# A recommendation model on one core: copied rows in a buffer per step, gathers that read the row numbers in place, and two more slots copied row by row

## What is computed

```python
x = jax.nn.relu(dense @ Wb0 + bb0)
x = jax.nn.relu(x @ Wb1 + bb1)
d = jax.nn.relu(x @ Wb2 + bb2)
sp = emb[jnp.arange(NUM_TABLES)[None, :], sparse_idx]
T = jnp.concatenate([sp, d[:, None, :]], axis=1)
Z = jnp.einsum('bnd,bmd->bnm', T, T)
li, lj = np.tril_indices(NUM_TABLES + 1, -1)
h = jnp.concatenate([d, Z[:, li, lj]], axis=1)
h = jax.nn.relu(h @ Wt0 + bt0)
h = jax.nn.relu(h @ Wt1 + bt1)
p = jax.nn.sigmoid(h @ Wt2 + bt2)
```

## Time and profile before

| quantity | value |
|---|---|
| median of three runs | 532.41 us |
| the profiled execution | 532.94 us |
| its span, first to last instruction | 530.9 us |
| outside the span | 2.0 us |
| POOL busy | 379.9 us (72%) |
| PE busy | 307.7 us (58%) |
| DVE busy | 245.5 us (46%) |
| ACT busy | 13.8 us (3%) |
| mean granted clock of TensorE | 0.72 |

### The profile page before, as it was taken

The page is one execution under the profiler, slowest core; times in us unless marked ns, Lnnn a source line. Parts: engine busy times, 40 slices in busy tenths (PEclk is TensorE's granted clock), DMA queues, the critical chain, the costliest instruction groups (busy, mean ns, idle before and its releaser), DMA issues.

```text
span 530.9 us, 12271 instructions
## 1 busy us (share of the span) xinstructions
PE 307.7 (58%) x3370; PEld 228.0 (43%) x3370; DVE 245.5 (46%) x375; ACT 13.8 (3%) x23; POOL 379.9 (72%) x406
## 2 busy tenths in 40 slices
PE   3799983774372732637436274366245744489776
PEld 1233432762262621626225252365124632377665
DVE  5435766644463344545246352376254732532220
ACT  1000000000000000000000000000000000021201
POOL 5777777777777777777777777777777777777710
PEclk9998895776667655777557775669567776579587
DMA  6445424444344433443344442444334443333310
GB/s 200 39 28 30 28 30 27 30 30 29 29 30 29 28 28 28 30 29 27 29 28 28 28 30 27 29 28 28 28 28 29 28 28 27 27 28 26 29 11 1
DMA packets 19968, 16.88 MB, mean 32 GB/s; under 512 B 11683, under 2 KB 12972, under 8 KB 19897
## 3 DMA queue, kind: packets, MB, share of 16 engines
q0 software_dynamic: 12800, 13.13, 31.8%
q1 hardware_dynamic: 4378, 2.68, 4.6%
q10 hardware_dynamic: 2732, 0.51, 3.4%
HBM read 16.28 MB, written 0.01 MB: 31 GB/s over the span
## 4 chain that ended last, share of the span: by engine, by line
POOL 50%; issue 20%; DMA 15%; PE 9%; DVE 6%; POOLq 0%; ACT 0%; DVEq 0%; ACTq 0%
POOL rows L307 50%; DMA rows<-in_emb,idx_step 14%; PE ps_t L343 3%; DVE vecs_mv L702 3%; PE ps_turn L351 1%; PE ps_turn L365 1%; PE ps_gram L334 1%; PE ps_feat L334 1%; PE ps_t L477 1%; DMA idx_raw<-in_idx 1%; PE ps_t L446 1%; PE ps_gram L419 1%; DVE hb L659 1%; DVE vecs_st L702 0%; PE ps_feat L446 0%
## 5 line engine op out<-in xcount | busy, mean ns | idle before, releaser
L307 POOL DMA_INDIRECT rows<-in_emb,idx_step x400 | 378.3, 946 | 126.3 <-issue 123.5
L365 PE MATMUL ps_turn<-ident,rows 128*128 128x128 f32 x182 | 41.3, 370 | 146.9 <-DMA rows<-in_emb,idx_step 138.2
L702 DVE COPY vecs_st<-ps_turn 128x512 f32<-128x512 f32 (+1 forms) x49 | 46.9, 958 | 117.2 <-PE ps_turn L365 116.8
L365 PEld LDWEIGHTS ps_turn<-ident,rows 128*128 128x128 f32 x182 | 27.8, 186 | 161.0 <-issue 145.0
L702 DVE COPY vecs_mv<-ps_turn 64x512 f32<-64x512 f32 (+1 forms) x98 | 96.2, 981 | 0.7
L397 PE MATMUL ps_gram<-vecs_mv,vecs_st 128*32 128x54 f32 x1792 | 40.6, 275 | 34.6 <-DVE vecs_mv L702 20.3
L397 PEld LDWEIGHTS ps_gram<-vecs_mv,vecs_st 128*32 128x32 f32 x1792 | 37.3, 156 | 39.6 <-DVE vecs_mv L702 23.1
L477 PE MATMUL ps_t<-wt_sb,ht_t 128*128 128x256 f32 x128 | 50.4, 562 | 0.0
L712 DVE STREAM_TRANSPOSE gram_s<-ps_gram 128x864 f32<-128x864 f32 x16 | 17.3, 1082 | 51.7 <-PE ps_gram L397 41.0
L477 PEld LDWEIGHTS ps_t<-wt_sb,ht_t 128*128 128x128 f32 x128 | 34.6, 284 | 14.5 <-issue 7.8
L446 PE MATMUL ps_t<-feat_t,wt_sb 117*128 117x128 f32 x192 | 38.2, 354 | 0.6 <-ACT feat_t L587 0.6
(11 more groups left out here) (57 smaller groups left out, 218.9 us busy)
## 6 DMA issues: line engine op xcount, KB each, us to landing
fetched<-in_emb SPq DMA_DIRECT2D x1024, 0.2 KB
fetched<-in_emb ACTq DMA_DIRECT2D x1024, 0.2 KB
rows<-in_emb,idx_step POOLq DMA_INDIRECT x400, 3.6
wt_sb<-in_wt SPq DMA_DIRECT2D x1, 1024.0 KB
wb_sb<-in_wb SPq DMA_DIRECT2D x1, 512.0 KB
wt_sb<-in_wt SPq DMA_DIRECT2D x1, 512.0 KB
idx_raw<-in_idx SPq DMA_DIRECT2D x1, 175.0 KB, 3.2
wt_sb<-in_wt ACTq DMA_DIRECT2D x1, 128.0 KB
```

Of the source, the lines that this page charges most:

```text
L307: nc.gpsimd.indirect_dma_start(rows[:, t, h * DIM:(h + 1) * DIM], None, emb_rows, bass.IndirectOffsetOnAxis(idx_step[:, c:c + 1], 0)).then ...
L365: turned = nc.tensor.transpose(ps_turn[r % 2][:, j, :], rows[:, first + j, :], ident[:, :])
L702: moved = nc.vector.tensor_copy(to, source)
```

## The change

The diff, cut to its core (the loops of ACT are as those of SP; the changes of `kernel()` fill the larger index array; the semaphores follow the code):

```diff
+EXTRA_STEPS = (2, 4)
+EXTRA_PARTS = ((0, 1), (2, 3))
+EXTRA_PLACE = 32
+FETCH_PARTS = EXTRA_PLACE + PARTS
...
-        idx_step = sb("idx_step", [P, STEP_COLS], I32)
-        fetched = sb("fetched", [P, 2, 2 * DIM])
+        fetched = sb("fetched", [P, STEPS, 3 * DIM])
...
+        def fetches(i, h):
+            own = [(h * PARTS + q, h + 1, q) for q in range(PARTS)]
+            return own + ([(EXTRA_PLACE + q, 0, q) for q in EXTRA_PARTS[h]] if i in EXTRA_STEPS else [])
...
-            sp.wait_ge(fetch_done, 4)
-            with sp.Fori(0, STEPS // 2) as k:
-                for side in range(2):
-
-                    sp.wait_ge(fetched_moved, k * 2 + (side + 1))
-                    for q in range(PARTS):
-                        places = load_places(mybir.EngineType.SP, 0, q, k * 2 + side)
-                        for j in range(PART):
-                            sp.dma_start(landing(side, 0, q * PART + j), emb_bytes[bass.ds(places[j], ROW_BYTES)])\
-                                .then_inc(fetch_landed[0][side][q // 2], 16)
+            sp.wait_ge(fetch_done, 5)
+            for i in range(STEPS):
+                for place, block, q in fetches(i, 0):
+                    places = load_places(mybir.EngineType.SP, place, i)
+                    for j in range(PART):
+                        sp.dma_start(landing(i, block, q * PART + j), emb_bytes[bass.ds(places[j], ROW_BYTES)])\
+                            .then_inc(fetch_landed[0][i], 16)
...
-            pool.sem_inc(fetched_moved, 2)
...
-                pool.wait_ge(staged, i + 1)
+                pool.wait_ge(idx_ready, 3 if i else 1 + (lo >= HEAD))
                 pool.wait_ge(rows_turned, i * NR + hi)
...
-                    bass.IndirectOffsetOnAxis(idx_step[:, c:c + 1], 0)).then_inc(landed, 16)
+                    bass.IndirectOffsetOnAxis(idx_row[:, c:c + 1], 0)).then_inc(landed, 16)
...
-            with pool.Fori(0, STEPS - 1) as i:
+            for i in range(STEPS - 1):
...
-                                gather(t, h, rows_landed[r])
+                                if (t, h) != (FETCHED - 1, 1):
+                                    gather(i, t, h, rows_landed[r])
+                                elif i not in EXTRA_STEPS:
+                                    gather(i, t, h, other_gathered)
...
-                pe.wait_ge(rows_landed[r], (i + 1) * (32 * GATHERED[r]))
+                pe.wait_ge(rows_landed[r], (i + 1) * (32 * GATHERED[r] if r < NR - 1 else 16))
...
-            def stage(i, staged, lo, hi, runs):
-
-                for r in runs:
-                    dve.wait_ge(rows_landed[r], (i + 1) * (32 * GATHERED[r]))
-                nc.vector.tensor_copy(idx_step[:, lo:hi], idx_row[:, bass.ds(i * STEP_COLS + (STEP_COLS + lo), hi - lo)])\
-                    .then_inc(staged, 1)
...
-            def move_fetched(i, side, nth):
+            def move_fetched(i):
                 for h in range(2):
-                    for q in range(PARTS // 2):
-                        dve.wait_ge(fetch_landed[h][side][q], nth * (32 * PART))
+                    dve.wait_ge(fetch_landed[h][i], 16 * PART * len(fetches(i, h)))
                 dve.wait_ge(rows_turned, i * NR + NR)
-                nc.vector.tensor_copy(rows[:, FETCHED, :], fetched[:, side, :]).then_inc(fetched_moved, 1)
+                if i in EXTRA_STEPS:
+                    moved = nc.vector.tensor_copy(rows[:, FETCHED - 1:, :].rearrange("p t c -> p (t c)")[:, DIM:], fetched[:, i, :])
+                else:
+
+                    dve.wait_ge(other_gathered, 16 * sum(n not in EXTRA_STEPS for n in range(min(i, STEPS - 2) + 1)))
+                    moved = nc.vector.tensor_copy(rows[:, FETCHED, :], fetched[:, i, DIM:])
+                moved.then_inc(fetched_moved, 1)
...
-            with dve.Fori(0, STEPS // 2 - 1) as k:
-                step(k * 2 + 1, 1, k + 1)
-                step(k * 2 + 2, 0, k + 2)
+            for i in range(1, STEPS - 1):
+                step(i)
```

More of the change, by code:

```diff
@@ L179, in build @@
         fetch_done = sem("fetch_done")
-        fetch_landed = [[[sem(f"fetch_landed{h}_{side}_{q}") for q in range(PARTS // 2)] for side in range(2)]
-                        for h in range(2)]
+        fetch_landed = [[sem(f"fetch_landed{h}_{i}") for i in range(STEPS)] for h in range(2)]
+        other_gathered = sem("other_gathered")
         fetched_moved = sem("fetched_moved")
@@ L238, in turned_half, with load_places @@
                     ps_turn[(h * NR + r) % 2][part, 0:n, :])
-        def load_places(engine, h, q, i):
+        def load_places(engine, p, i):
             _, places = nc.values_load_multi_w_load_instructions(
-                fetch_at[h * PARTS + q:h * PARTS + q + 1, bass.ds(i * PART, PART)], engines=(engine,),
+                fetch_at[p:p + 1, i * PART:(i + 1) * PART], engines=(engine,),
                 min_val=0, max_val=(TABLES * VOCAB - 1) * ROW_BYTES,
@@ L326, in _ @@
                         for t in range(first, first + GATHERED[r]):
-                            gather(t, h, rows_landed_last[h][r])
+                            gather(STEPS - 1, t, h, rows_landed_last[h][r])
         @block.tensor
@@ L624, in _ @@
             nc.scalar.activation(probs[:, 0:1], ones[:, 0:1], ACT.Sigmoid).then_inc(table_ready, 1)
[L626 to L635, removed]
+            act.wait_ge(fetch_done, 5)
+            for i in range(STEPS):
+                for place, block, q in fetches(i, 1):
+                    places = load_places(mybir.EngineType.Activation, place, i)
+                    for j in range(PART):
+                        act.dma_start(landing(i, block, q * PART + j), emb_bytes[bass.ds(places[j], ROW_BYTES)])\
+                            .then_inc(fetch_landed[1][i], 16)
             act.wait_ge(d_ready, CHUNKS)
@@ L766, in first_step, with step @@
                     spread(0, 2 * (c - FIRST_CHUNKS) + 3)
-                move_fetched(0, 0, 1)
-                stage_rest(0)
+                move_fetched(0)
                 spread(0, NR - 1)
                 products(0)
-            def step(i, side, nth):
+            def step(i):
                 spread(i, 0)
@@ L800, in last_step @@
                 logit(i - 1, 1)
-                move_fetched(i, i % 2, STEPS // 2)
+                move_fetched(i)
                 spread_last(0, 5)
@@ L819, in _ @@
                 nc.vector.tensor_scalar(neg, raw, 0, VOCAB, ALU.is_lt, ALU.mult).then_inc(idx_done, 1)
-                dve.wait_ge(idx_done, n * 3 + 1)
+                dve.wait_ge(idx_done, n * 2 + 1)
                 nc.vector.scalar_tensor_tensor(out=raw, in0=raw, scalar=VOCAB - 1, in1=neg,
                                                op0=ALU.min, op1=ALU.add).then_inc(idx_done, 1)
-                dve.wait_ge(idx_done, n * 3 + 2)
+                dve.wait_ge(idx_done, n * 2 + 2)
                 if n == 0:
                     dve.wait_ge(base_ready, 1)
-                    for to, staged, a, b in ((idx_step, head_staged, 0, HEAD_COLS), (idx_step, rest_staged, HEAD_COLS, hi)):
-                        nc.vector.scalar_tensor_tensor(out=to[:, a:b], in0=raw[:, a:b], scalar=0, in1=idx_base[:, a:b],
-                                                       op0=ALU.max, op1=ALU.add).then_inc(staged, 1)
-                nc.vector.scalar_tensor_tensor(out=idx_row[:, lo:hi], in0=raw, scalar=0, in1=idx_base[:, lo:hi],
-                                               op0=ALU.max, op1=ALU.add).then_inc(idx_done, 1)
+                for a, b in ((lo, HEAD_COLS), (HEAD_COLS, hi)) if n == 0 else ((lo, hi),):
+                    nc.vector.scalar_tensor_tensor(out=idx_row[:, a:b], in0=idx_raw[:, a:b], scalar=0, in1=idx_base[:, a:b],
+                                                   op0=ALU.max, op1=ALU.add).then_inc(idx_ready, 1)
                 if n == 0:
@@ L839, in _ @@
                     dve.wait_ge(fetch_done, 2)
-                    nc.vector.tensor_scalar(neg, raw, 0, FETCHED * VOCAB, ALU.max, ALU.add).then_inc(fetch_done, 1)
-                    dve.wait_ge(fetch_done, 3)
+                    for a, b, table in ((0, EXTRA_PLACE, FETCHED), (EXTRA_PLACE, FETCH_PARTS, FETCHED - 1)):
+                        nc.vector.tensor_scalar(neg[a:b], raw[a:b], 0, table * VOCAB, ALU.max, ALU.add).then_inc(fetch_done, 1)
+                    dve.wait_ge(fetch_done, 4)
                     nc.vector.tensor_scalar(at, neg, ROW_BYTES, None, ALU.mult).then_inc(fetch_done, 1)
@@ L881 @@
     idx = by_step(get("r_sparse_idx"), (4, 0, 1, 3, 5, 2), (1, 0, 2, 3, 5, 4)).reshape(P, STEPS, TABLES, 2)
+    fetch_idx = np.zeros((FETCH_PARTS, STEPS * PART), idx.dtype)
+    for place, t, h in ((0, FETCHED, 0), (PARTS, FETCHED, 1), (EXTRA_PLACE, FETCHED - 1, 1)):
+        fetch_idx[place:place + PARTS] = idx[:, :, t, h].reshape(PARTS, PART, STEPS).transpose(0, 2, 1).reshape(PARTS, -1)
     arrays = {
```

45 lines of the change are left out of this document (18 added, 27 removed).

## The result

The changed kernel took 549.32 us (median of four runs, 548.28 to 549.99), the kernel before 532.4 us. The ratio is 1.030, with a 95% interval of 1.026 to 1.034. Forecast were 551 us and 1.034. The profiled run took 548.28 us, with a span of 545.4 us; 2.9 us lie around it, in place of 2.0.

A forecast was written before the change was run, and what follows sets the result against it. POOL's gathers were taken as the bound, with copies crowding one DMA engine; step 7's move at 504, plus 44.1 - 0.6 + 1.5, gave a 549 us span, with 2.0 around it 551 us; 8-in-10 range 536 to 561.

The forecast's parts named there:

- The main step: Copies served at 4.70 a us; the last lands by 504 us and holds DVE's move of step 7 until then.
- The gain: On POOL: two gathers fewer (2.5 us) and no wait for `idx_step` in step 5 (0.9 us), sum 3.4 us.
- this stop: POOL waits in the last step for the turned run, ahead of its 17th gather, near 461 us, some 8 us.
- the same number comes by a second way: Gathers' lateness grows to 27 us at step 6's end; its last run is turned near 468, giving 502 us.
- one of my signs: Sign that would show the forecast: gathers in step 6 land 27 us and more after issue.
- the first way: From the served rate of 4.70 copies a us: the last copy lands at 504 us, which delays step 7's move.
- ACT's late start: ACT issues its last copy at 477 us, so its part of the last step starts 6 us late.
- The issue bounds: Rival: the issue of copies, not the engine, limits; lateness stops growing; 536 to 541 us; chance 0.17.
- Faster: POOL decides: Rival: POOL's gain of 3.4 us arrives in full; 529.5 us; chance 0.06.
- The pile-up spreads: Rival: gathers 30 us late stop POOL in steps 5 and 6 too, or its queue fills; 558 to 565 us; chance 0.12.

The follow-up runs named there:

- three runs at 539 to 540 us: Changed kernel with one extra slot, 540.06 us; with step 6's rows moved in step 7, 538.91 us; with step 7's copies reordered, 539.02 us.
- 17 slots: Changed kernel with one extra slot (step 2) in place of two: 540.06 us, ratio 1.010 against the kernel before.
- the other order: Changed kernel, 18 slots kept, step 7's copies issued lower half first, upper half behind on SP: 539.02 us, ratio 1.008 against the kernel before.
- 16 slots: Changed kernel with no extra slots (2048 copies, 400 gathers): 533.2 us against 533.45 for the kernel before, ratio 1.000.

## Why the prediction was right

**The main step held, with its size.** Forecast were a served rate of 4.70 copies a us and the last landing by 504. It came at 502.6, which makes 1717 copies in 362.1 us from 140.5 on, 4.74 a us. The move of step 7 stood at 502.68, and that of step 4, expected from a landing at 342, at 344.79. From the move to the end 44.1 - 0.6 + 1.5 = 45 us were forecast and 42.7 came. That the clock would be lower behind the wait is seen only in part: the stretch from 503 to 524 had 0.63, where the like stretch before had 0.67. The landing was 1.3 us early, the tail 2.3 us short and the time around the span 0.9 us more than forecast, which makes 548.28 us for the profiled run out of 551.

```profile
503.00:524.00 21.00, 15.40 (x322) 13.39 (x323) 5.95 (x8) 4.72 (x7) 1.02 (x2) 0.63 0.06 6
```

**The gain was there and worth little.** The last gather started 2.5 us earlier, not 3.4: the two gathers and the hole at step 5 are gone (3.4 us), the start was 0.5 us earlier, and a new stop of POOL in step 7 took 1.5 us: from 459.43 to 462.14 in place of 1.25.

```profile
459.43 0.94 POOL L313 DMA_INDIRECT rows<-in_emb,idx_row  x1 [0.30 <-issue]
462.14 0.94 POOL L313 DMA_INDIRECT rows<-in_emb,idx_row  x1 [1.77 <-issue]
```

I had put this stop at the right place, near 461, but at 8 us. The run that it waits for was turned at 460.66, not at 468.

**What was off: "the same number comes by a second way".** That step carried the lateness on by 0.054 us a us to 27 us at the end of step 6. It stopped at 20.6, so one of my signs (gathers that land 27 us and more after issue) didn't come, though SP's last copies themselves were 26.6 us late. So the last run of step 6 came at 460, not 468, and the move would have been ready at 491.3, not 502. The two ways weren't two proofs of one number but two costs of different size: the late landing of copies, 549 us, and the late gathers, 539 us. The first hides the second, as three runs at 539 to 540 us showed. For the forecast it made no difference, as the later of two waits decides. It did in the experiments, where I twice expected about 530 us once the landing was out of the way (17 slots, and the other order). The forecast stood on the first way alone.

**ACT's late start** was forecast at 477 and came at 479.31. As DVE's move was ready only at 491.3 and copies landed at 502, it decided nothing in the changed kernel. The runs at 539 to 540 us came out the same with ACT's copies done at 452 and at 479.6 us, so it wasn't the second cost either.

**The rivals.** "The issue bounds" fell with the run without ACT's copies: same issue on SP, 529.95 us. "Faster: POOL decides" is what that run shows, and it needs the crowding gone. "The pile-up spreads" (POOL stopped in steps 5 and 6) didn't come. The issue did slow down late (0.413 us a copy for 0.386), but the end was set by the landing, 24 us behind the last issue.

## What to carry to other kernels

Where one queue is relieved by moving work to others, look at what those share with it behind the issue: here two copy queues and a share of every gather met at one server that was already late, which the landing times showed (10.5, 15.3, 16.9, 20.7 us) while every busy share looked harmless. A buffer for each step takes away waits. Here the lateness had fallen during them, from 20.7 to 9.8 us, and without them the wait came at the last consumer, once there were more copies than could be served in time; with 16 slots free running cost and gained nothing. And when a crowded resource delays two consumers, price both chains: taking away the longer one wins only the difference, here 549 to 539 us and not to 530.

## What was not expected of the hardware

- The crowding isn't in proportion: 2.5 copies a us beside the gathers leave them at 2.5 us, 4.7 a us put them at 20.6.
- One sixteenth of a gather alone is late: fifteen updates of its semaphore come within 2.5 us of its issue and the sixteenth 20.6 us after it.
- The gathers' lateness stops at 20.6 us from step 3 on, though the copies go on falling behind: the last copies landed 23.7 (ACT) and 26.6 us (SP) after their issue, and SP's issue slowed by 7%. What holds the gathers at this value is open.
- The same two programs took 532 and 549 us on some chips, 876 and 889 us on others, where SP issued copies at less than half its pace while gathers were issued, and a move between registers on SP took up to 1409 ns.

The Trainium skill (DMA: Bandwidth & Descriptors, section "Why a DMA increments its semaphore by 16 and not by 1") gives a copy of a single element, here one row on one partition, one engine, and for SP and ACT alike the lowest-numbered one. The trace agrees with the form: it has each row copy as one element of 256 bytes. The traces agree with one shared engine by the one late update out of sixteen and by the run without ACT's copies; which engine it is no run here shows.
